# The full attention core with each second score as four products of 32 keys

## The reference, cut to what matters

```
q = (x @ Wq.T).reshape(B, S, H, Hd)        # H = 16, Hd = 8
k = (x @ Wk.T).reshape(B, S, H, Hd)
v = (x @ Wv.T).reshape(B, S, H, Hd)
energy = jnp.einsum('bqhd,bkhd->bhqk', q, k)
attn = jax.nn.softmax(energy / jnp.sqrt(jnp.float32(D)), axis=-1)
out = jnp.einsum('bhqk,bkhd->bqhd', attn, v)
```

## Time and profile before

| | us |
|---|---|
| three runs | 2834.13, 2838.63, 2847.8 |
| median | 2838.63 |
| span of the profiled execution | 2837.6 |
| full attention core, from its first slot to its last product (480 to 1206 us of the span) | 726 |
| of these, steps with second scores (526 to 1206) | 680 |

### The profile page before, as it was taken

One profiled execution on the slowest core, in us unless ns is written; L12 is line 12 of the kernel. 1 busy time (PEld: TensorE's weight loads), 2 busy tenths in 40 slices (PEclk: granted clock), 3 DMA queues, 4 the chain that ended last, 5 costly groups with the idle time before them and its releaser, 6 DMA issues. The chain is left out here.

```text
span 2837.6 us, 44598 instructions
## 1 busy us (share of the span) xinstructions
PE 2394.6 (84%) x15629; PEld 1114.6 (39%) x15674; DVE 1850.6 (65%) x2753; ACT 1566.3 (55%) x3173; POOL 639.1 (23%) x1194
## 2 busy tenths in 40 slices
PE   5986566799999999869996899999687887886778
PEld 2543343122222222147774233333346645744633
DVE  5644666899999999231115777777386476547577
ACT  2542452488888888733333467777457546633321
POOL 4860000000000000000001122222175256402356
PEclk8986777799999999979997799999898998987889
DMA  3210003312012111000001222221010010010000
GB/s 92 77 45 0 11 1 98 62 50 50 26 50 50 28 47 27 2 6 1 1 1 54 72 65 60 73 56 46 23 35 22 1 31 5 2 29 2 2 0 16
DMA packets 62296, 93.48 MB, mean 33 GB/s; under 512 B 25299, under 2 KB 37749, under 8 KB 62074
## 3 DMA queue, kind: packets, MB, share of 16 engines
q1 hardware_dynamic: 54330, 86.02, 11.4%
q10 hardware_dynamic: 7744, 4.59, 0.8%
HBM read 75.87 MB, written 10.49 MB: 30 GB/s over the span
## 5 line engine op out<-in xcount | busy, mean ns | idle before, releaser
L933 DVE TENSOR_REDUCE l1a_core_mpart<-l1a_core_psA 128x1 f32<-128x1024 f32 x512 | 601.5, 1220 | 67.9 <-PE l1a_core_psA L848 67.9
L915 ACT ACTIVATE l1a_core_prob<-l1a_core_psB 128x512 f32<-128x512 f32 x1024 | 551.3, 596 | 131.9 <-PE l1a_core_psB L861 130.0
L1275 ACT ACTIVATE l2a_core_prob<-l2a_core_psB 128x384 f32<-128x384 f32 (+3 forms) x656 | 303.8, 525 | 157.3 <-PE l2a_core_psB L1213 152.1
L1300 DVE TENSOR_REDUCE l2a_core_mpart<-l2a_core_psA 128x1 f32<-128x1024 f32 (+4 forms) x352 | 292.0, 879 | 60.2 <-PE l2a_core_psA L1197 58.8
L872 PE MATMUL l1a_core_psV<-l1a_core_prob,l1a_core_vh 128*32 128x512 f32 x2048 | 275.3, 610 | 0.1
L861 PE MATMUL l1a_core_psB<-l1a_core_qh,l1a_core_kh 75*128 75x512 bf16 x640 | 194.9, 387 | 0.5 <-ACT l1a_core_prob L915 0.5
L1229 PE MATMUL l2a_core_psV<-l2a_core_prob,l2a_core_vh 128*32 128x256 f32 (+3 forms) x1856 | 175.7, 433 | 0.5
L2130 DVE SCALAR_TENSOR_TENSOR X<-l1e_psO,W,X 128x128 f32<-128x128 f32 x128 | 36.0, 344 | 194.7 <-PE l1e_psO L2078 194.7
L2113 ACT ACTIVATE l1e_h<-l1e_psH,l1e_w_b 128x512 f32<-128x512 f32 x128 | 87.5, 687 | 136.6 <-PE l1e_psH L2071 136.6
L1142 POOL TENSOR_SCALAR_AFFINE_SELECT l2a_core_prob<-l2a_core_prob 128x128 f32<-128x128 f32 x256 | 74.5, 294 | 337.2 <-ACT l2a_core_prob L1275 333.4
L2078 PEld LDWEIGHTS l1e_psO<-l1e_w_w,l1e_h 128*128 128x128 f32 x1024 | 118.7, 192 | 13.4 <-issue 13.4
(11 more groups left out here) (677 smaller groups left out, 4417.6 us busy)
## 6 DMA issues: line engine op xcount, KB each, us to landing
l2f_tab<-in_rotary SPq DMA_DIRECT2D x32, 128.0 KB, 2.1
l0a_core_qh<-qparts SPq DMA_DIRECT2D x36, 96.0 KB
l0a_core_kh<-kparts SPq DMA_DIRECT2D x36, 96.0 KB
l1a_core_qa<-qparts SPq DMA_DIRECT2D x32, 96.0 KB
l1a_core_ka<-kparts SPq DMA_DIRECT2D x32, 96.0 KB
l2a_core_qa<-qparts SPq DMA_DIRECT2D x32, 96.0 KB
l2a_core_ka<-kparts SPq DMA_DIRECT2D x32, 96.0 KB
l1a_core_qh<-qparts SPq DMA_DIRECT2D x30, 96.0 KB
```

What stands on the lines that cost most here:

```text
L915: nc.scalar.activation(prob[u % (2 * PER_KB)][:], psB[u % 3][:], ACT.Exp, scale=scale).then_inc(b_exped, 1)
L933: nc.vector.tensor_reduce(mpart[:, n // 2, n % 2:n % 2 + 1], psA[i % 2][:], AX.X, ALU.max).then_inc(a_freed, 1)
L1275: nc.scalar.activation(prob[n % RING][:, 0:cols], psB[n % 3][:, 0:cols], ACT.Exp, scale=scale).then_inc(b_exped, 1)
L1300: ins = nc.vector.tensor_reduce(mpart[:, place, part:part + 1], psA[i % 2][:, lo * P:hi * P], AX.X, ALU.max)
```

## The change

Each second score is issued as four products of 32 weight columns (32 keys) in place of one of 128. Each of the four reads the same 75 by 512 query operand and writes its 32 partitions of the same psB bank. The first still waits for the exponential three before, the last signals ACT. Everything else is as it was.

```
+COLS = 32
+COL_TILES = P // COLS
...
-                mm(psB[u % 3][:], kh[h % 3][0:QKM_ROWS, kb * P:(kb + 1) * P], qh[h % 3][0:QKM_ROWS, c * CH:(c + 1) * CH],
-                   start=True, stop=True).then_inc(b_scored, 1)
+                for j in range(COL_TILES):
+                    lo = kb * P + j * COLS
+                    ins = mm(psB[u % 3][j * COLS:(j + 1) * COLS, :], kh[h % 3][0:QKM_ROWS, lo:lo + COLS],
+                             qh[h % 3][0:QKM_ROWS, c * CH:(c + 1) * CH], start=True, stop=True, skip_group_check=True)
+                ins.then_inc(b_scored, 1)
```

## The result

The changed kernel takes 2806.4 us in the median of four runs against 2836.4 before: 0.9884 of the time (95% interval 0.986 to 0.9908), 1.2% faster. The two medians lie 30 us apart; the ratio stands for 33 us, and its interval for 26 to 40. (The 2836.4 holds a fourth run beside the three given above.) I had forecast 2823 and a range from 2807, so the measured time lies just outside it, on the fast side. The direction and the half that DVE takes back were right. The saving on PE was twice what I had summed.

The account below looks back on a forecast made before the run. PE was taken to set the pace, with DVE close behind at zero margin. 237 steps at 0.055 gave 13.0 us, plus 3.0 for 19 steps, less 0.5: 15.5 us off 2838.6, so 2823, range 2807 to 2842.

Parts of the forecast that it names:

- the half that DVE takes back: First scores' second pair stays 2.84 us behind the previous step's first pair; of 0.11 us saved, 0.055 a step remains.
- The saving on PE: Full attention core: start-to-start changes at a step's places, summed to -0.11 us of PE a step.
- the surcharge: Extra 0.08 to 0.09 us between PE starts where product shape changes, four places a step; claimed to hang on shape.
- The rival that it stays: Extra time hangs on type or tile written, not shape; 18 us slower, 2857; chance 0.07.
- The rival in which DVE gives way: At the first scores DVE's chain yields, so the whole 0.11 us a step arrives: 29 us, 2809.5; chance 0.13.
- I take 0.24: Second scores: four 32-column bf16 products together take 0.24 us, priced from a first-layer values round of 256 f32 columns.
- 0.45: Values to second score: 0.45 us after the change, for 0.54 before.
- The first score's place: Second score to first score: 0.34 us after the change, for 0.31 before (+0.03).
- The round of rows 8: First layer's core: values round of 256 f32 columns, four 32-column products, 0.24 us from round to round.
- The bounds I had drawn: Second scores' four products at 0.23 with half kept give 2818; first score's shape change moves 12 us either way.
- Two signs in the profile: First scores' weight loads wait for DVE some 13 us more in all; DVE still idle in each step.
- The rival that four products overlap only in part: Second scores' four products run longer: gain gone at 0.27 us, 2872 at 0.30, 3507 without overlap; chance 0.12.

Follow-up runs that it names:

- each half of the change: Against the kernel before, only chunks 2 and 3 (values' side) as products of 32 keys: 0.9961 of its time; only chunks 0 and 1 (first scores' side): 0.9965.
- the 64 keys: Every second score as two products of 64 keys, against the kernel before: 1.0031 of its time.
- DVE's work halved: Changed kernel with DVE taking maxima over only the first 512 columns of each slot: 0.9752 of the time before; the same on the kernel before: 0.992.
- the window core: Second scores as products of 32 keys also in the third layer's causal core and first layer's window core, added to the changed kernel: 0.981 of the time before.

## Why the prediction was right or wrong

**Right: what the surcharge hangs on.** The rival that it stays, whatever the shape, is refuted by the places into and out of the values, each half of the change moving only its own, and by the 64 keys.

**Right: half comes back at the first scores.** T = (2.84 + PE's own part) / 2 holds in the changed kernel and in its two halves. Averaged over the steps of each trace that hold no transposition, PE's own part is 2.162, 2.265 and 2.294 us and the step is 2.505, 2.555 and 2.574, where the formula gives 2.501, 2.553 and 2.567. A step set by DVE's own pace would have been the same in all three. With 64 keys PE's own part is 2.41, and with 0.23 inside the pair it sets the step alone, at 2.64. Over the 13 heads from the second to the fourteenth the changed kernel is 0.109 a step faster on average (2.634 to 2.525), half of 0.22 to 0.23. The rival in which DVE gives way gave a better time, 2809.5, but that is luck: it adds the whole of a saving that was summed at half its size, and its mechanism is refuted, since the other half appears only with DVE's work halved.

**Wrong: the size of the step on PE.** The term was -0.11 us; it measured -0.22. "I take 0.24" for four products was 0.21 to 0.23, and "0.45" for the values' rounds was 0.43 to 0.44. The first score's place, "0.34", was 0.32. Over the six places, with the rows of the changed step, the overstatement is 0.03 + 0.02 + 0.01 + 0.03 + 0.01 + 0.02 = 0.12. Less 0.01 at the place from first to second score (0.32, where I had left 0.31), that is 0.11, the missing part. The round of rows 8 and the first round of rows 5 both stand directly behind a change of shape, and I carried their price to rounds that have none ahead of them. The half-changes show it for the values: 0.43 when entered in their own shape, 0.45 when not. The trace of the kernel before shows it for the f32 rounds of 256 columns that I priced from. Two rounds of the first layer, the first of which starts after PE has stood idle:

```profile
81.58 0.42 PE L622 MATMUL l0a_core_psV<-l0a_core_prob,l0a_core_vh 128*32 128x256 f32 x4 [0.19 <-POOL l0a_core_prob L545]
...
81.80 0.42 PE L622 MATMUL l0a_core_psV<-l0a_core_prob,l0a_core_vh 128*32 128x256 f32 x4
```

Here it is 0.22 from round to round, not 0.24. So my row was the dearer of two kinds in the same trace. Second scores of 32 keys take 0.23 behind the first scores and 0.21 or 0.22 behind products of their own shape. The bounds I had drawn (0.23 for four products, 2818) were thus too narrow: they varied one price and left the values' own at 0.45. Two signs in the profile were off as well: the loads of first scores wait for DVE 43.5 us longer in all, not 13, and DVE is no longer idle in each step, but in 91 of some 210 (the list of waits above).

**Right: the rest.** The rival that four products overlap only in part is refuted: they take 0.21 to 0.23 us, no longer than one product of 128 keys. Issue is no limit: twelve more products and loads a step fit into less time. The overhead of 60 cycles a matmul in the Trainium skill ("TensorEngine Tiling (Array Packing)", Performance Considerations, Instruction Overhead) would have made the step longer; the trace does not show it, with four products in 0.21 to 0.23 us. The steps without first scores fell from 2.40 to 2.18, where I had said 2.24. In the timeline of PE in the last head, from 1140.63 to 1142.81:

```profile
1140.63 0.82 PE L865 MATMUL l1a_core_psB<-l1a_first_qh,l1a_first_kh 75*32 75x512 bf16 x12
...
1141.94 1.03 PE L877 MATMUL l1a_core_psV<-l1a_core_prob,l1a_core_vh 128*32 128x512 f32 x8
1142.81 0.82 PE L865 MATMUL l1a_core_psB<-l1a_first_qh,l1a_first_kh 75*32 75x512 bf16 x12
```

The sum with measured terms: 237 x 0.109 = 25.8, 19 x 0.22 = 4.2, together 30.0 of the 32.5 us. The rest may lie around the last slot, where the clock differed (below); no run shows that by itself.

## What to carry to other kernels

Read the distance of starts on PE at each place where the tile shape changes; if two neighbours can be cut into one shape on the column groups, each such place gives about 0.1 us. Cut only where it joins shapes: 64 columns beside 32 gained nothing, and in the window core it only moved the change. Count the places that gain a change of shape along with those that lose one. Before counting the gain, look for a wait whose margin is zero: here a tie over two steps of PE's order took half, and it stood in the list of waits with only 7 us. And price a product from a row that has the same neighbour ahead of it.

## What was not expected

The values' first round is 0.02 us longer when it is entered straight through a change of shape (0.45 against 0.43). In the first layer the same holds for rounds of 256 columns, and it is gone where PE stood idle ahead of the round. What makes it so, these runs leave open.

Behind the last slot, once PE has waited for the last maxima, the granted clock can be at its lower level, 1.2 GHz, for a while. Windows of the kernel with the change on the values' side only: the stretch around that place, the wait itself, and what follows it:

```profile
1120.00:1160.00 40.00, 38.15 (x269) 8.66 (x267) 20.03 (x20) 28.56 (x54) 0.83 (x4) 0.80 0.01 1
1140.00:1144.00 4.00, 2.15 (x23) 0.57 (x19) 1.62 (x4) 2.17 (x5) 0.83 (x4) 1.00 0.00 0
1144.00:1164.00 20.00, 20.00 (x100) 3.65 (x96) 0.00 (x0) 11.88 (x24) 0.00 (x0) 0.50 0.03 5
```

PE is busy 2.15 of 4 us, and then runs 20 us at the lower level. From 1120 to 1160 us the mean is 0.80 here, 0.92 in the kernel before, and 1.00 in the changed kernel. So some us of difference between kernels can arise there that no edit of the steps explains.
